# A decoder layer whose first layer norm is folded into the second and whose expert weights come from a tanh

## What is computed

```python
x = layernorm(x + mamba(x))                 # first layer norm ("LN1")
x = layernorm(x + retention(q=x, kv=ctx))   # second ("LN2")
x = layernorm(x + moe(x))                   # third ("LN3")
# mamba: xz = x @ W_in; causal conv of 4 taps, silu; a scan over the positions with 16 states
#        per channel; y = ys * silu(z); y @ W_out
# retention: q = xpos(x @ Wq), k = xpos(ctx @ Wk), v = ctx @ Wv; ((q k^T) * decay_mask) v
# moe: logits = x @ router_w.T + bias; the top 2 of 16 experts, weighed by a softmax of the two;
#      hidden = silu(x @ gate) * (x @ up); plus a shared expert
# layernorm(x) = (x - mean) / sqrt(var + 1e-5)
```

## Time and profile before

| what | us |
|---|---|
| median of 3 runs | 1212.84 (1212.56 to 1213.9) |
| the profiled execution, its own time | 1216.39 |
| its span, first to last instruction | 1214.6 |
| mean granted TensorE clock in it | 0.967 of full speed |
| PE busy | 1080.0 |
| DVE busy | 1093.3 |
| ACT busy | 997.8 |
| POOL busy | 989.8 |

### The profile page before, as it was taken

How to read it: one execution, slowest core, us unless ns; L and a number is a source line. 1 busy time by engine, 2 the same in 40 slices (tenths; PEclk the granted TensorE clock), 3 DMA queues, 4 the chain that set the end, 5 groups by cost and what they waited for, 6 DMA issues and landing times.

```text
span 1214.6 us, 18948 instructions
## 1 busy us (share of the span) xinstructions
PE 1080.0 (89%) x6049; PEld 766.0 (63%) x6049; DVE 1093.3 (90%) x1598; ACT 997.8 (82%) x2288; POOL 989.8 (81%) x623
## 2 busy tenths in 40 slices
PE   5677888989999898999989898998989899988897
PEld 2455666666666766666666666666666667666565
DVE  2899999999999999999999999999999999999523
ACT  5677888989888898988889898988889898888343
POOL 0587797979988897998888799888979888898844
PEclk9687999999999999999999999999999999999999
DMA  6344454545464454546455444645444465454221
GB/s 181 141 164 154 142 174 150 187 141 182 158 202 158 159 183 143 188 150 209 150 169 173 159 173 153 206 160 173 159 172 161 157 204 165 159 179 158 70 80 58
DMA packets 84116, 194.55 MB, mean 160 GB/s; under 512 B 17288, under 2 KB 47936, under 8 KB 67632
## 3 DMA queue, kind: packets, MB, share of 16 engines
q1 hardware_dynamic: 84016, 193.33, 47.3%
HBM read 179.14 MB, written 5.77 MB: 152 GB/s over the span
## 4 chain that ended last, share of the span: by engine, by line
ACT 34%; DVE 26%; PE 24%; issue 11%; POOL 3%; DMA 0%; SPq 0%; DVEq 0%; POOLq 0%; ACTq 0%
ACT decay L680 15%; PE bank L283 14%; DVE state L822 14%; DVE drive_bank L720 6%; PE y_bank L287 6%; ACT L680 4%; ACT silu L656 2%; PE down_bank L283 2%; PE bank L287 2%; ACT L636 1%; ACT L648 1%; ACT L656 1%; POOL hid L916 1%; ACT x_rows L526 1%; POOL read L873 1%
## 5 line engine op out<-in xcount | busy, mean ns | idle before, releaser
L873 POOL TENSOR_TENSOR read<-state,bc_all 128x1024 f32<-128x1024 f32 x256 | 605.4, 2365 | 162.4 <-DVE state L822 139.0
L822 DVE TENSOR_TENSOR_SCAN state<-decay,drive_bank 128x512 f32<-128x512 f32 x512 | 593.9, 1200 | 0.0
L680 ACT ACTIVATE decay<-delta,a_neg 128x252 f32<-128x252 f32 x1024 | 420.4, 494 | 0.8
L720 DVE TENSOR_TENSOR drive_bank<-dx_bank,bc_all 128x512 f32<-128x512 f32 x512 | 327.3, 685 | 0.3 <-DVE state L822 0.3
L287 PE MATMUL y_bank<-ident,read 128*128 128x128 f32 x2048 | 285.7, 287 | 40.4 <-POOL read L873 40.3
L287 PEld LDWEIGHTS y_bank<-ident,read 128*128 128x128 f32 x2048 | 246.2, 148 | 90.6 <-POOL read L873 57.6
L916 POOL TENSOR_TENSOR hid<-gu,comb_all 128x512 f32<-128x512 f32 (+1 forms) x136 | 165.0, 1213 | 20.1 <-DVE gu L837 16.6
L283 PE MATMUL down_bank<-down_w,hid 128*128 128x128 f32 x1024 | 140.9, 280 | 15.1 <-POOL hid L916 12.6
L656 ACT ACTIVATE silu<-bank 128x512 f32<-128x512 f32 (+1 forms) x153 | 87.3, 571 | 81.4 <-PE bank L283 79.6
L283 PEld LDWEIGHTS down_bank<-down_w,hid 128*128 128x128 f32 x1024 | 127.0, 191 | 38.0 <-POOL hid L916 28.6
L837 DVE TENSOR_TENSOR gu<-silu,bank 128x512 f32<-128x512 f32 (+1 forms) x136 | 86.8, 638 | 56.7 <-PE bank L283 30.0
(11 more groups left out here) (126 smaller groups left out, 1496.3 us busy)
## 6 DMA issues: line engine op xcount, KB each, us to landing
bc_all<-bc_dram SPq DMA_DIRECT2D x128, 1024.0 KB, 4.9
comb_all<-comb_dram SPq DMA_DIRECT2D x240, 128.0 KB, 4.5
x_in<-in_x_dram SPq DMA_DIRECT2D x15, 256.0 KB, 6.0
ctx_in<-in_ctx_dram SPq DMA_DIRECT2D x15, 256.0 KB, 5.2
k_pair<-k_pair SPq DMA_DIRECT2D x30, 128.0 KB, 2.1
q_pair<-q_pair SPq DMA_DIRECT2D x30, 128.0 KB, 2.0
out_dram<-y_out SPq DMA_DIRECT2D x15, 256.0 KB, 5.6
comb_all<-comb_dram SPq DMA_DIRECT2D x32, 64.0 KB, 2.7
```

Source lines behind the costliest of these rows:

```text
L680: done = e.activation(seqs(decay_t[j % DECAYS][:, i, h, :])[:, :, 1:T], seqs(delta[c % 2][:, h, sub * SUB:(sub + 1) * SUB])[:, :, 1:T], AC ...
L720: e.tensor_tensor(drive_bank[:, n, :, :], dx_bank[:, :, :], bc_all[group % BC_BUFS][:, 0, PAIR * i + n, :].unsqueeze(1).to_broadcast([P, H ...
L822: e.tensor_tensor_scan(one(state_t[j % STATE_BUFS], n), one(decay_t[j % DECAYS], n), one(drive_bank, n), 0.0, ALU.mult, ALU.add).then_inc( ...
L873: e.tensor_tensor(read_t[j % READS][:, :, :, :], state_t[j % STATE_BUFS][:, :, :, :], bc_all[group % BC_BUFS][:, 1, PAIR * i:PAIR * (i + 1 ...
```

## The change

It has four parts.

1. **LN1 is gone.** PE makes the residual with features on the partitions: three matmuls of 512 columns (`center`, and `w_out` twice) in place of twelve of 128. ACT copies the bank out as `x1T`, not normalised, and takes its square (`r1_sq`) in one instruction each. The rows `x1`, their squares by blocks, the POOL pair of LN1, the scaling by blocks and the four transposes are gone. q is made at PE's old place of the transposes, and its copy on ACT follows the third silu (tick 82, before it stood at slot 44).
2. **The lost scale comes back in the epsilon.** PE multiplies `r1_sq` by a column of 1e-5 (`r1_var_mm`, a matmul with 2 columns for each block), ACT copies that out plus 1e-10 (`r1_var`), and POOL adds it to LN2's variance in place of the constant. `square` now scales by 128^-0.5, so that the sum of squares is the variance.
3. **The router's weights** are 0.5 +- 0.5 tanh(difference / 2). DVE has two tensor_scalar and one weighing of both one-hot rows, where it had a tensor_scalar, a reciprocal, a product and two weighings. ACT has Tanh for Exp.
4. **The order is a table.** Slots become ticks, two per slot, and the stages look their ticks up in `AT`. On SP, and on POOL and DVE but for the edited operations, the order is the old one. On PE two things move: the scores stand one y sum earlier, and q one scan step earlier. `until` is written anew in ticks: it is 2 for up (1.7 slots before), 3 for the residual (4.5 slots before), and `r1_var` takes a bank that nothing took before.

```diff
-                if (c := chunk_at(slot, 36, 33)) is not None:
-                    bank = take(("out", c), slot, 4.5)
-                    w.wait_ge(S["yT"], subs_after(c))
+                for c in due(tick, "out_mm"):
+                    bank = take(("out", c), tick, 3)
                     w.wait_ge(S["centered"], 1)
-                    for q in range(blocks_of(c)):
-                        cols = slice(q * P, (q + 1) * P)
-                        mm(bank.t[:, cols], xT[c % 3][:, cols], center[:, :], stop=False)
-                        for h in range(HALVES):
-                            done = mm(bank.t[:, cols], y_gatedT[:, h, cols], w_out[:, h, :], start=False,
-                                      stop=h == HALVES - 1)
+                    mm(bank.t[:, 0:width(c)], center[:, :], xT[c % 3][:, 0:width(c)], stop=False)
+                    w.wait_ge(S["yT"], subs_after(c))
+                    for h in range(HALVES):
+                        done = mm(bank.t[:, 0:width(c)], w_out[:, h, :], y_gatedT[:, h, 0:width(c)], start=False,
+                                  stop=h == HALVES - 1)
                     done.then_inc(S["out_mm"], 1)
-                    bank.free = (NORMED[LN1], at(c))
+                    bank.free = (S["r1_sq"], at(c))
...
+                for c in due(tick, "r1_var_mm"):
+                    bank = take(("r1_var", c), tick, 2)
+                    w.wait_ge(S["r1_sq"], at(c))
+                    w.wait_ge(S["zero"], DECAYS + 2)
+                    for q in range(blocks_of(c)):
+                        done = mm(bank.t[:, 2 * q:2 * q + 2], r1_sq[:, q * P:(q + 1) * P], eps_col[:, :])
+                    done.then_inc(S["r1_var_mm"], 1)
+                    bank.free = (S["r1_var"], at(c))
...
-                        bank = take((name, c, index), slot, 1 if name == "gate" else 1.7)
...
+                    bank = take(("gate", c, index), tick, 2)
...
+                    bank = take(("up", c, index), tick, 2)
...
-                if (c := chunk_at(slot, 36, 33)) is not None:
+                for c in due(tick, "x1T"):
                     w.wait_ge(S["out_mm"], at(c))
-                    w.wait_ge(S["x1T_mm"], at(c - 1))
-                    square(bank_of["out", c][:, :], x1, LN1, c)
-                if (c := chunk_at(slot, 38, 35)) is not None:
-                    normalise(bank_of["out", c][:, :], x1, LN1, c)
...
+                    copy(x1T[:, 0:width(c)], bank_of["out", c][:, 0:width(c)]).then_inc(S["x1T"], 1)
+                    w.wait_ge(S["r1_var_mm"], at(c - 1))
+                    e.activation(r1_sq[:, 0:width(c)], bank_of["out", c][:, 0:width(c)], ACT.Square, scale=D ** -0.5).then_inc(
+                        S["r1_sq"], 1)
...
+                for c in due(tick, "r1_var"):
+                    w.wait_ge(S["r1_var_mm"], at(c))
+                    w.wait_ge(VAR_EPS[LN2], at(c - 1))
+                    of_block = bank_of["r1_var", c][:, 0:2 * blocks_of(c)].rearrange("p (q i) -> p q i", i=2)
+                    e.activation(r1_var[:, 0:blocks_of(c)], of_block[:, :, 0], ACT.Copy, bias=LN_EPS * LN_EPS,
+                                 scale=1.0).then_inc(S["r1_var"], 1)
...
+                    elif op in (13, 14):
+                        w.wait_ge(S["top_tanh"], at(c))
+                        done = e.tensor_scalar(soft[:, op - 11, 0:n], soft[:, 1, 0:n], 0.5 if op == 13 else -0.5, 0.5, ALU.mult, ALU.add)
+                    elif op == 15:
+                        w.wait_ge(S["combT_mm"], at(c - 1))
+                        done = e.tensor_tensor(rank[:, :, 0:n, :], comb[:, 0:2, 0:n, :],
+                                               soft[:, 2:4, 0:n].unsqueeze(3).to_broadcast([P, 2, n, EXPERTS]), ALU.mult)
```

More of the change, by code:

```diff
@@ L31 @@
 LN_EPS = 1e-5
-PER = 32
 PAIR = 2
@@ new lines, in decoder_layer @@
+        DUE = {name: {} for name in AT}
+        for name, places in AT.items():
+            for n, (normal, last) in enumerate(places):
+                due_of(name, n, normal, last)
+        EXP_DUE = {}
+        for j in range(STEPS):
+            half, n = divmod(j, SUB_STEPS)
+            virtual, sub = divmod(half + 1, SUBS)
+            step = SUB_STEPS * sub + n
+            place = SUB_TICKS * (SUBS * virtual - 1) + (EXP_AT[step] if virtual < CHUNKS - 1 else LAST_EXP_AT[step])
+            EXP_DUE.setdefault(place, []).append(j)
@@ L301, in _ @@
                     bank.free = (S["xT"], at(c))
[L302 to L303 removed]
+                for c in due(tick, "tap_mm"):
+                    bank = take(("xb", c, 0), tick, 3)
                     w.wait_ge(S["xT"], at(c))
@@ L364, in _ @@
                     bank.free = (S["ctxT"], at(c))
-                if (c := chunk_at(slot, 35, 35)) is not None:
-                    bank = take(("k", c), slot, 1)
+                for c in due(tick, "k_mm"):
+                    bank = take(("k", c), tick, 2)
                     w.wait_ge(S["ctxT"], at(c))
@@ L370, in _ @@
                     bank.free = (S["k_copy"], at(c))
-                if (c := chunk_at(slot, 36, 35)) is not None:
-                    bank = take(("v", c), slot, 1)
+                for c in due(tick, "v_mm"):
+                    bank = take(("v", c), tick, 2)
                     w.wait_ge(S["ctxT"], at(c))
@@ L413, in _ @@
+                for c in due(tick, "q_mm"):
+                    bank = take(("q", c), tick, 2)
                     w.wait_ge(S["x1T"], at(c))
@@ L443, in _ @@
                     bank.free = (S["x2T"], at(c))
-                if (c := chunk_at(slot, 63, 56)) is not None:
-                    bank = take(("router", c), slot, 1.5)
+                for c in due(tick, "router_mm"):
+                    bank = take(("router", c), tick, 3)
                     w.wait_ge(S["x2T"], at(c))
@@ L452, in _ @@
                     bank.free = (S["router"], at(c, 0, ROUTER))
-                if (c := chunk_at(slot, 68, 60)) is not None:
-                    bank = take(("combT", c), slot, 1)
+                for c in due(tick, "combT_mm"):
+                    bank = take(("combT", c), tick, 2)
                     w.wait_ge(S["comb"], at(c))
@@ L525, in square @@
                 for q in range(blocks_of(c)):
-                    done = e.activation(out[:, q, :], blocks(bank)[:, q, :], ACT.Square, scale=1.0,
+                    done = e.activation(out[:, q, :], blocks(bank)[:, q, :], ACT.Square, scale=D ** -0.5,
                                         accum_out=squares[i][:, q:q + 1])
@@ L828, in _ @@
+                    done.then_inc(S["comb" if op == 16 else "router"], 1)
+                for c, index in due(tick, "gu"):
                     total = TILES * c + index
@@ L907, in _ @@
                                     ALU.mult).then_inc(S["ret"], 1)
-                for index, (where, last) in enumerate(zip(FFN_AT, LAST_FFN_AT)):
-                    if index == 0 or (c := chunk_at(slot, where + 2, last + 2)) is None:
-                        continue
-                    use = PAIRS * c + index - 1
+                for c, pair in due(tick, "hid"):
+                    index = pair + 1
+                    use = PAIRS * c + pair
                     w.wait_ge(S["gu"], at(c, index, TILES))
```

579 lines of the change are left out of this document (300 added, 279 removed).

## The result

The changed kernel takes 1241.03 us (median, 1238.68 to 1241.82) where the kernel before takes 1212.71 (1212.56 to 1213.9): a ratio of 1.0228, 95% interval 1.021 to 1.0246. It is slower, as forecast, but by 28 us and not by 7; the range ended at 1230. The profiled execution has a span of 1239.5 us, 24.9 more than before. That is less than 28.3, because the profiled execution of before was itself 3.7 us above the median of its kernel and this one 0.6. An execution can also be some per cent longer at a lower clock throughout; such executions are left out of all times here, and as the only profile of e6 is of one, only e6's time is used.

The account below looks back on a forecast made before the run. DVE was taken to bound the middle. 12 chunks x 0.7 = 8.4, + 1.3 + 0.3 - 2.7 = +7.3 us on the median of 1212.84 gave 1220.1, told as 1220.0; range 1207 to 1230.

Parts of the forecast that it names:

- both hazards: PE's middle list: up 3 waits for its own gate's silu (+0.9); scores (1.09) precede gate 4; together +0.7 us a chunk.
- The relief of ACT: ACT saves about 1.3 us a chunk, but waits that much longer for PE ahead of a silu: no gain.
- PE's clock: TensorE's granted clock below 2.4 GHz cost DVE 1.0 us once, at `gu` 6, in 8 of 14 chunks.
- q's move: On PE, q made a scan step earlier delays a y sum by 0.43 where PE waits for reads anyway: 0.
- The relief of DVE: Reciprocal and joined weighing save 0.27 a chunk, the wait ahead of `hid` 0 to 0.18: at most 0.45 us.
- The ends: Outside the 12 middle chunks: +1.3 for one chunk's expert tiles, +0.3 first chunk, -2.7 in the last chunk.
- the first router's stretch: Last chunk, PE's waits of 2.24 for `x_rows` and 0.17 for `combT` ahead of the shared expert: 1.6 us gained.
- The second router: In the last chunk, the second router and its two table loads give 0.5 us.
- the stretch ahead of the first `logits`: In the last chunk, the stretch bound by POOL before the router gives 0.6 us.
- The other two stretches: Expert tiles in a full chunk's scan, hit once by `r1_var` and up 4's silu: +1.3; the 256-wide first chunk: +0.3.
- rival D: PE's clock falls in fewer chunks, as 12 short matmuls become 3 long: 1208 to 1213 us; chance 0.12.
- Rival C: PE's clock falls in more chunks, if PE has more gaps: 1226 to 1236 us; chance 0.13.

Follow-up runs that it names:

- e6: Changed kernel with the scores back behind gate and up of expert index 4, and the 8-row `dt` matmuls padded to 128 rows with zeros: 1221.72 us.
- e1: Changed kernel with the scores back behind the y sum, gate and up of expert index 4, old place in the last chunk, same banks: 1240.34 us.
- e4: Changed kernel with scores back, `r1_var` copied early, and in full chunks the banks from the old `until` numbers for up and residual: 1230.42 us.
- e7: Changed kernel in the order and banks of before: q and its copy at their old place, `r1_var` in the transposes' places: 1222.75 us.
- e8: e7 with `r1_var`'s matmuls ahead of gate 5, its copy later, the square behind silu 0, and `dt` matmuls padded to 128 rows: 1203.28 us.
- e3: Kernel before with the tanh router alone: 1212.07 us, ratio 0.9979 to the kernel before.
- e12: Kernel before with the `dt` matmuls padded to 128 rows and the tanh router: 1202.08 us, ratio 0.9898 to the kernel before.
- e10: Changed kernel with only the `dt` matmuls padded from 8 to 128 rows with zeros: 1238.00 us, ratio 1.0195 to the kernel before.
- e2: Changed kernel with up of index 3 in `r1_var`'s bank, copied earlier, and up 4 of the last full chunk in its own bank: 1244.72 us.
- e9: Kernel before with six unused 128x128 multiplications added to DVE behind each chunk's router: 1239.04 us, ratio 1.0205 to the kernel before.

## Why the prediction was wrong

**Right.** The mechanism and its place: both hazards are there, worth 0.8 and 0.5 to 0.6 a chunk, the wait at `gu` 4 grew from 1.15 to 2.41 (told: 2.3), up 3 waits for its own gate's silu by 0.69 (told: 0.9), and it is slower. The relief of ACT shows as a longer wait for PE (1.42 ahead of silu 1 before, 2.23 after), as told. That PE's clock is a term of its own was told as well.

**The step that failed first** is the one that costed q's move at nothing: "That q is made a scan step earlier costs a y sum 0.43 of delay where PE waits for reads anyway: 0." Before, the profile shows no wait of PE from 627.39 to 648.25 us. It is full into gate 3, so the 0.37 that q's matmul takes more than the transposes is paid; ACT gets q's copy (0.5) ahead of the copy of `xT`, and PE waits for that copy, another 0.44 by its step. The sum of the steps began with gate 3 at its old time. By the clean chunk:

| step | clean chunk | worth | told |
|---|---|---|---|
| after | 71.67 | | |
| scores behind gate and up 4 (e1) | 70.89 | 0.78 | 0.7 for both |
| up 3 off its gate's bank (e4) | 70.35 | 0.54 | |
| q and its copy at the old place, `r1_var` in the transposes' (e7) | 70.05 | 0.30 | 0 |
| `r1_var` and the square off PE's and ACT's full stretch (e8) | 69.59 | 0.46 | 0 |

Each step is the difference to the row above, and e4 and e7 changed some other banks too. The sum is 2.08 where 0.7 was told. The two hazards of 0.9 and 1.09 were set against a slack of 1.6, which the 0.92 in front of gate 3 had already used by more than half.

**The relief of DVE** was told as 0.45 a chunk and taken off the path. e3 and e12 show that it never reaches it: the wait ahead of `hid` 0 takes it, and in the changed kernel DVE's busy time in a chunk did not even fall (67.42 before, 67.51 after). The statement that this wait goes "since up of the shared expert no longer waits" was wrong, since silu 0 is there no sooner; it is 0.16 after. In e8, with the square behind silu 0, it does go, and a wait of 0.38 at `y_gated` for PE takes its place.

**The ends** were told at -1.1 and came to +10.6. Only the first router's stretch is as told: the wait for `x_rows` went, `soft` has a wait of 0.34 instead of 1.25, and from the first `logits` (23.94 later than before) to the next `hid` 0 (21.64 later) 2.3 us were gained, told as 1.6. The second router, told at 0.5, gained 0.06. What was missed is, first, the last chunk's own numbers in the table: the scores moved there too, from 90 to 86, ahead of gate 3, where POOL hasn't made k yet. DVE's and PE's timelines after:

```profile
1201.24 0.69 DVE L880 TENSOR_TENSOR gu<-silu,bank 128x512 f32<-128x512 f32 x1 [5.94 <-PE bank L354]
```

```profile
1198.74 0.68 PE L354 MATMUL bank<-q_t,k_t 128*128 128x128 f32 x4 [2.00 <-POOL k_t L939]
```

and before:

```profile
1176.43 0.69 DVE L837 TENSOR_TENSOR gu<-silu,bank 128x512 f32<-128x512 f32 x1 [3.25 <-PE bank L283]
```

That gives 2.7 back at once. Second, in the last chunk's scan the scores of the chunk before wait 1.90 for q, which POOL ends at 1159.14, ahead of a y sum and gate 4, and these run at a low clock (granted 0.57 from 1160 to 1164 us), so the stretch ahead of the first `logits`, told as a gain of 0.6, lost 2.0:

```profile
1159.24 1.19 PE L354 MATMUL bank<-q_t,k_t 128*128 128x128 f32 x8 [1.90 <-issue]
```

e1, with the scores back, has 3.25 at that `gu` 3 again, and all that follows the last full chunk's mark takes 5.0 us less (165.0 for 169.9).

The other two stretches, +5.5 and +2.1, were told as 1.3 and 0.3. (The 1.3 belongs to the expert tiles that run in the last full chunk's scan; the prediction calls them the first full chunk's.) The hazards strike harder there than in the middle, but a good part is the clock. DVE's timeline in the last full chunk's scan, where `gu` 3, 4 and 6 waited 0, 1.23 and 0 before, and the granted clock at its end (columns of the earlier trace rows):

```profile
1082.31 0.69 DVE L880 TENSOR_TENSOR gu<-silu,bank 128x512 f32<-128x512 f32 x1 [1.20 <-issue]
...
1090.67 0.69 DVE L880 TENSOR_TENSOR gu<-silu,bank 128x512 f32<-128x512 f32 x1 [2.82 <-issue]
...
1112.06 0.69 DVE L880 TENSOR_TENSOR gu<-silu,bank 128x512 f32<-128x512 f32 x1 [2.40 <-ACT silu L718]
```

```profile
1104.00:1108.00 4.00, 3.94 (x18) 3.20 (x19) 4.00 (x6) 2.76 (x5) 2.00 (x2) 0.70 0.55 213
```

So the changed kernel does have falls of the clock behind its `dt` matmuls, at the ends, where the kernel before has none. In e10, padded, the 2.40 is 0.61, and this stretch takes 72.4 for 74.5. The first chunk is alike: `gu` 4 waits 3.03 for 0.59, and `gu` 6 waits 1.78 for none, behind 4 us at a clock of 0.50 (172 to 176 us), while the 138 us ahead of its first expert tile came out 2.2 shorter.

**The clock** went in the middle as rival D had it, with eight stretches fewer, and about 10 us came back from it; some of that went again in the falls at the ends. At an equal clock the change costs 34.5 us where 7.3 was told; with the clock left free it is 28.3, so the clock hid some 6 us of the error, and that is luck. Rival C is what e1, e2 and e7 show: another order, and nine or ten falls, some of 2.63. Why the changed kernel has none in 12 chunks stays open. e9 speaks against the period alone. The wait between the two `dt` matmuls is 0.57 both in the changed kernel and in e1, which has nine falls, so it isn't that either; what TensorE does ahead of `dt` was changed by itself in no run.

**Table loads.** DVE's timeline at `soft` in the last full chunk's router, before and after:

```profile
1162.77 0.17 DVE L804 TENSOR_SCALAR soft<-soft 128x4 f32<-128x4 f32 x1 [1.25 <-ACT soft L669]
```

```profile
1185.81 0.38 DVE L861 TENSOR_SCALAR soft<-soft 128x4 f32<-128x4 f32 x2 [0.34 <-ACT soft L731]
```

With the load of 1.28 gone, the wait is 0.9 shorter. The further 1.4 that the Trainium skill ("ScalarE: Activation LUTs", section "What ACT_TABLE_LOAD costs") adds for the drain did not show here.
